# One-hots of a graph score pass from squares: VectorE compares on broadcast rows become TensorE products and ScalarE Relu

## The reference, cut to what matters

```python
Q, K = enh @ Wq + bq, enh @ Wk + bk          # one row per node
mod_k  = K[src] + 0.2 * rel_w[edge_relations][:, None, :]
scores = einsum('ehd,ehd->eh', Q[dst], mod_k) / D ** 0.5
```

## Time and profile before

| | |
|---|---|
| median of three runs | 2750.49 us (2748.61 to 2753.2) |
| span of the profiled execution, first to last instruction | 2465.8 us |
| busy in the span | PE 86%, DVE 73%, POOL 60%, ACT 35% |
| score pass, by window 214.00 to 1294.50 | 1080.5 us |
| TensorE clock granted in the score pass, mean | 0.83 |
| bytes moved in the score pass | 348 GB/s |

### The profile page before, as it was taken

The page is one execution under the profiler, slowest core; times in us unless marked ns, Lnnn a source line. Parts: engine busy times, 40 slices in busy tenths (PEclk is TensorE's granted clock), DMA queues, the critical chain, the costliest instruction groups (busy, mean ns, idle before and its releaser), DMA issues. The chain is left out here.

```text
span 2465.8 us, 50459 instructions
## 1 busy us (share of the span) xinstructions
PE 2121.3 (86%) x11360; PEld 1390.5 (56%) x11361; DVE 1790.9 (73%) x3103; ACT 863.0 (35%) x2796; POOL 1476.9 (60%) x1460
## 2 busy tenths in 40 slices
PE   6994888888888888888856999999789999779996
PEld 3542444444444444444425877777655555468885
DVE  6666999999999999999957777888776665331111
ACT  3541111111111111111106777777535555432221
POOL 3665777777777777777731777777664441024342
PEclk9996888888888888888868999999989999889998
DMA  5666999999999999999995988888534552465451
GB/s 174 210 208 187 358 360 358 365 354 359 364 354 352 358 360 359 354 360 358 359 207 194 315 278 282 278 278 280 195 128 154 194 192 104 162 234 183 151 178 42
DMA packets 387966, 649.65 MB, mean 263 GB/s; under 512 B 40218, under 2 KB 235806, under 8 KB 387780
## 3 DMA queue, kind: packets, MB, share of 16 engines
q1 hardware_dynamic: 309812, 386.36, 46.9%
q0 software_dynamic: 77824, 262.55, 30.2%
q10 hardware_dynamic: 272, 0.00, 0.0%
HBM read 470.87 MB, written 178.83 MB: 263 GB/s over the span
## 5 line engine op out<-in xcount | busy, mean ns | idle before, releaser
L758 POOL DMA_INDIRECT s_kv<-kv_d,s_index x832 | 793.3, 953 | 266.0 <-issue 247.4
L890 PE MATMUL s_q_ps<-q,s_is_dst 128*128 x2496 | 470.7, 303 | 155.1 <-DVE s_key L812 142.5
L1390 PE MATMUL a_sum_ps<-a_w,a_is_dst 128*128 128x260 f32 x1760 | 402.9, 387 | 20.9 <-DVE sums L1361 11.9
L1303 POOL TENSOR_TENSOR a_w<-a_v,a_w 128x512 f32<-128x512 f32 x220 | 299.1, 1365 | 164.6 <-ACT a_w L1260 109.7
L1390 PEld LDWEIGHTS a_sum_ps<-a_w,a_is_dst 128*128 128x128 f32 x1760 | 327.4, 190 | 96.4 <-issue 26.0
L890 PEld LDWEIGHTS s_q_ps<-q,s_is_dst 128*128 128x128 bf16 x2496 | 200.6, 102 | 285.4 <-issue 226.7
L808 DVE TENSOR_TENSOR s_key<-s_kv,s_rel_ps 128x1024 f32<-128x1024 f32 x208 | 252.5, 1214 | 53.1 <-DMA s_kv<-kv_d,s_index 46.5
L1276 ACT ACTIVATE a_w<-a_v,a_w 128x64 f32<-128x64 f32 x1100 | 285.8, 335 | 2.8 <-DMA a_v<-v_d 2.8
L1337 DVE SCALAR_TENSOR_TENSOR a_is_dst<-node_of,first_node,a_col_ps 128x256 f32<-128x256 f32 x440 | 208.5, 475 | 83.0 <-PE a_sum_ps L1390 65.8
L817 DVE TENSOR_REDUCE s_part<-s_key 128x16 f32<-128x1024 f32 x208 | 253.7, 1220 | 10.7
L812 DVE TENSOR_TENSOR s_key<-s_key,s_q_ps 128x1024 f32<-128x1024 f32 x208 | 253.8, 1220 | 7.2
(11 more groups left out here) (312 smaller groups left out, 2942.1 us busy)
## 6 DMA issues: line engine op xcount, KB each, us to landing
a_v<-v_d SPq DMA_DIRECT2D x440, 256.0 KB, 3.7
v_d<-s_kv SPq DMA_DIRECT2D x208, 512.0 KB, 8.2
s_local<-local_d SPq DMA_DIRECT2D x106, 256.0 KB
...
s_kind<-type_d SPq DMA_DIRECT2D x212, 64.0 KB
s_kv<-kv_d,s_index POOLq DMA_INDIRECT x832
kv_d<-pkv SPq DMA_DIRECT2D x50, 256.0 KB, 2.0
...
```

What stands on the lines that cost most here:

```text
L758: nc.gpsimd.indirect_dma_start(out=kv[:, g * GROUP + b, :], out_offset=None, in_=R["kv"], in_offset=bass.IndirectOffsetOnAxis(ap=index[:, ...
L890: nc.tensor.matmul(q_ps[b][:, u, :], is_dst[:, h, e], M["q3"][:, bass.ds(regs[g % GROUPS * GROUP + u], 1), j, :] .rearrange("p a c -> p (a ...
L1303: nc.gpsimd.tensor_tensor(heads(w[:, at, mine, 0:C]), heads(v[:, g, mine, :]), w[:, at, mine, C:, None].broadcast_to([P, len(tiles), H, D] ...
L1390: ins = nc.tensor.matmul(sum_ps[(g * PAIRS + k) % BANKS][:], is_dst[:, g % WRING, 2 * k + u, :], w[:, g % WRING, 2 * k + u, :], start=(u = ...
```

## The change

Neither `local` nor `type` is broadcast any more. The identity used is relu(1 - (lane - value)^2), which for whole numbers is 1 where they are equal and 0 elsewhere. The square is written as lane^2 - 2 lane value + value^2, and value^2 is split into a bf16 part and its rest, so that three bf16 rows per number (`terms`: high square, low square, value) carry it exactly. TensorE multiplies these rows (6 partitions, `s_marks`, both numbers together) by a constant matrix `M["mark"]` into `s_off_ps`, and ScalarE applies Relu with the bias `M["slack"]` = 1 - lane^2.

- `stage_weights`: 14 small VectorE instructions make `mark` and `slack`.
- `stage_tiles`: the rows for both numbers are squares and rests, made by DVE, ACT and POOL; 6 rows per 8 tiles are stored, 624 KB for each number, instead of 208 KB.
- `stage_scores`: VectorE's compares are gone. SP fetches 12 KB of `s_marks` for 8 tiles (four sets in flight), instead of 384 KB. Per group, PE makes two more products of 512 columns (`mark_kind`, `mark_dst`) and ACT two Relu of 128x512. `s_rel_ps` and `s_off_ps` are one buffer each: each mark waits until ACT has read the one before, and the relation product waits until DVE's add of the group before has read `s_rel_ps` (`key_added`). The first two relation parts are stacked on 128 partitions, so a tile has 2 relation products (L976 with 128 rows, L977 with 64) instead of 3. ACT's indices come one or two groups later, and its squares of the mixer are spread over two groups.

```diff
@@ stage_weights, VectorE @@
+            lane, a_dst, b_dst, a_kind, b_kind = M["lane"][:], *(coef[:, j:j + 1] for j in range(4))
+            st.mark(nc.vector.tensor_scalar(a_dst, lane, 1.5, None, ALU.is_lt))
+            st.mark(nc.vector.tensor_scalar(b_dst, lane, 2.0, -2.0, ALU.is_equal, ALU.mult))
...
+            st.mark(nc.vector.tensor_tensor(M["slack"][:, 0:1], lane, lane, ALU.mult))
+            st.mark(nc.vector.tensor_tensor(M["slack"][:, 1:2], M["lane64"][:], M["lane64"][:], ALU.mult))
...
+            st.mark(nc.vector.tensor_scalar(M["slack"][:], M["slack"][:], -1.0, 1.0, ALU.mult, ALU.add))
+            st.settle()
+            st.mark(nc.vector.tensor_scalar(M["mark"][:, 0, :], M["col"][:], b_dst, a_dst, ALU.mult, ALU.add))
+            st.mark(nc.vector.tensor_scalar(M["mark"][:, 1, :], col64[:], b_kind, a_kind, ALU.mult, ALU.add))
+            st.settle()
...
-            for j, part in enumerate((rel_1, rel_2, rel_3)):
-                st.mark(nc.vector.tensor_copy(M["rel3"][:, j, :], part[:]))
+            st.mark(nc.vector.tensor_copy(M["rel3"][0:NREL, 0, :], rel_1[0:NREL, :]))
+            st.mark(nc.vector.tensor_copy(M["rel3"][NREL:, 0, :], rel_2[NREL:, :]))
+            st.mark(nc.vector.tensor_copy(M["rel3"][0:NREL, 1, :], rel_3[0:NREL, :]))
 
@@ stage_tiles: SyncE, GpSimd, VectorE, ScalarE @@
-            for name, tile, ready in (("type", type_b, "type_set"), ("local", local_b, "local_stored")):
-                sp.wait_ge(S[ready], 1)
-                sp.dma_start(R[name][0:TS_ROWS, :], tile[:]).then_inc(S["stored"], 16)
-                sp.dma_start(R[name][TS_ROWS:, :], tile[0:2, :]).then_inc(S["stored"], 16)
+            for lo, ready in ((0, "near"), (MARK, "type")):
+                sp.wait_ge(S[ready + "_high"], 2)
+                sp.wait_ge(S[ready + "_low"], 1)
+                part = slice(lo, lo + MARK)
+                sp.dma_start(R["rows"][0:TS_ROWS, part, :], terms[:, part, :]).then_inc(S["stored"], 16)
+                sp.dma_start(R["rows"][TS_ROWS:, part, :], terms[0:4, part, :]).then_inc(S["stored"], 16)
...
+            pool.wait_ge(S["type_set"], 1)
+            nc.gpsimd.tensor_tensor(type_sq[:], type_f[:], type_f[:], ALU.mult).then_inc(S["type_squared"], 1)
+            pool.wait_ge(S["type_squared"], 1)
+            pool.wait_ge(S["type_high"], 2)
+            nc.gpsimd.tensor_tensor(term(MARK + 1), type_sq[:], term(MARK), ALU.subtract).then_inc(S["type_low"], 1)
...
+            nc.vector.tensor_scalar(near[:], local[:], -1.0, float(P), ALU.max, ALU.min).then_inc(S["near_set"], 1)
+            dve.wait_ge(S["near_set"], 1)
+            nc.vector.tensor_tensor(near_sq[:], near[:], near[:], ALU.mult).then_inc(S["near_squared"], 1)
...
+            dve.wait_ge(S["near_squared"], 1)
+            dve.wait_ge(S["near_high"], 2)
+            nc.vector.tensor_tensor(term(1), near_sq[:], term(0), ALU.subtract).then_inc(S["near_low"], 1)
...
-            nc.scalar.copy(by_tile(type_b), field(2)).then_inc(S["type_set"], 1)
+            nc.scalar.copy(type_f[:], field(2)).then_inc(S["type_set"], 1)
+            act.wait_ge(S["near_squared"], 1)
+            nc.scalar.copy(term(0), near_sq[:]).then_inc(S["near_high"], 1)
+            nc.scalar.copy(term(2), near[:]).then_inc(S["near_high"], 1)
...
-            act.wait_ge(S["local_set"], 1)
-            nc.scalar.copy(by_tile(local_b), local[:]).then_inc(S["local_stored"], 1)
+            act.wait_ge(S["type_squared"], 1)
+            nc.scalar.copy(term(MARK), type_sq[:]).then_inc(S["type_high"], 1)
+            nc.scalar.copy(term(MARK + 2), type_f[:]).then_inc(S["type_high"], 1)
@@ stage_scores @@
-        rel_ps = [ctx.enter_context(nc.psum_tensor(f"s_rel_ps{b}", [P, 2 * GROUP, D], F32)) for b in range(2)]
+        rel_ps = ctx.enter_context(nc.psum_tensor("s_rel_ps", [P, 2 * GROUP, D], F32))
+        off_ps = ctx.enter_context(nc.psum_tensor("s_off_ps", [P, GROUP * P], F32))
...
-                sp.dma_start(local[:, h, :], row(R["local"], n)).then_inc(rows_in[h], 16)
-                for k in range(2):
-                    sp.dma_start(kind[k * NREL:(k + 1) * NREL, h, :],
-                                 R["type"][bass.ds(n, 1), k * GROUP * P:(k + 1) * GROUP * P]
-                                 .broadcast_to([NREL, GROUP * P])).then_inc(rows_in[h], 16)
-
-            def block_in(n):
-                sp.dma_start(xnt[:], R["xnt"][bass.ds(n, 1)].rearrange("a p c -> (a p) c")).then_inc(xnt_in, 16)
-
-            for h in range(2):
+                sp.dma_start(marks[:, h, :], R["rows"][bass.ds(n, 1)].rearrange("a k e -> (a k) e")).then_inc(rows_in[h], 16)
+
...
-                act.wait_ge(gathered[g], (i + 1) * (16 * GROUP))
+                act.wait_ge(gathered[g], i * (16 * GROUP))
                 act.nop(nofuse=True)
-                indices(g, i + 1)
+                indices(g, i)
+
+            def hot_dst(m, count):
+                act.wait_ge(S["marked"], count)
+                act.nop(nofuse=True)
+                nc.scalar.activation(is_dst[:, m % 2, :], off_ps[:], ACT.Relu, bias=M["slack"][:, 0:1], scale=-1.0
+                                     ).then_inc(S["hot_ready"], 1)
...
+                for g in range(RING):
+                    n, at = i * 2 + g // 4 + 1, (i * RING + g) * 2
+                    hot_kind(g + 1, at + 4)
+                    if g % 4 == 1:
+                        square_keys(n)
+                    if g % 4 == 2:
+                        square_values(n)
+                    if g % 4 == 3:
+                        values(n)
+                        deviation(n)
+                    hot_dst(g + 2, at + 5)
+                    if g < 2:
+                        next_indices(g + RING - 2, i)
+                    elif more:
+                        next_indices(g - 2, i + 1)
+                    if g % 2 == 0 and g > 0:
+                        scores(g // 2 - 1, i)
...
-            def onehots(h, n):
-
-                dve.wait_ge(rows_in[h], n)
-                nc.vector.tensor_scalar(is_dst[:, h, :], local[:, h, :], M["lane"][:], None, ALU.is_equal)\
-                  .then_inc(S["steps"], 1)
-                nc.vector.tensor_scalar(is_kind[:, h, :], kind[:, h, :], M["lane64"][:], None, ALU.is_equal)\
-                  .then_inc(S["onehot_ready"], 1)
-
...
+            def mark_dst(m, seen):
+
+                pe.wait_ge(S["hot_ready"], seen)
+                pe.nop(nofuse=True)
+                nc.tensor.matmul(off_ps[:], M["mark"][0:2 * MARK, 0, :],
+                                 marks[:, m // 2 % SETS, m % 2 * GROUP * P:(m % 2 + 1) * GROUP * P],
+                                 start=True, stop=True).then_inc(S["marked"], 1)
...
+                    b, at = g % 2, i * RING + g
                     if g % GROUPS == 0:
                         regs = load_row(pe, at_block, M["blk"][0:1, bass.ds((i * RINGS + g // GROUPS) * SLOTS, SLOTS)], RBLK - 1)
-                    if b == 0:
-                        pe.wait_ge(S["onehot_ready"], i * (RING // 2) + g // 2 + 1)
-
-                    pe.wait_ge(S["qr_free"], i * RING + g + 1)
+                    mark_kind(g + 1, at * 2 + 3)
+
+                    pe.wait_ge(S["qr_free"], at + 1)
                     pe.nop(nofuse=True)
                     for u in range(GROUP):
-                        e = slice((b * GROUP + u) * P, (b * GROUP + u + 1) * P)
+                        e = slice(u * P, (u + 1) * P)
                         for j in range(3):
-                            nc.tensor.matmul(q_ps[b][:, u, :], is_dst[:, h, e],
+                            nc.tensor.matmul(q_ps[b][:, u, :], is_dst[:, b, e],
                                              M["q3"][:, bass.ds(regs[g % GROUPS * GROUP + u], 1), j, :]
                                              .rearrange("p a c -> p (a c)"), start=(j == 0), stop=(j == 2))
-                        half = slice(b * NREL, (b + 1) * NREL)
-                        for j in range(3):
-                            ins = nc.tensor.matmul(rel_ps[b][:, u, :], is_kind[half, h, u * P:(u + 1) * P],
-                                                   M["rel3"][half, j, :], start=(j == 0), stop=(j == 2))
+
+                    if g % 2 == 0:
+                        pe.wait_ge(rows_in[(g + 2) // 2 % SETS], (i + 1 + (g + 2) // RING) * 16)
+                    mark_dst(g + 2, at * 2 + 4)
+
+                    pe.wait_ge(S["key_added"], at + RING)
+                    pe.nop(nofuse=True)
+                    for u in range(GROUP):
+                        e = slice(u * P, (u + 1) * P)
+                        nc.tensor.matmul(rel_ps[:, u, :], is_kind[:, b, e], M["rel3"][:, 0, :], start=True, stop=False)
+                        ins = nc.tensor.matmul(rel_ps[:, u, :], is_kind[0:NREL, b, e], M["rel3"][0:NREL, 1, :],
+                                               start=False, stop=True)
```

136 lines of the change are left out of this document (81 added, 55 removed).

## The result

The changed kernel takes 3018.85 us, median of 4 runs (3007.98 to 3024.06), beside 2751.84 us (2748.61 to 2756.59) for the kernel before: a ratio of 1.0967, 95% interval 1.0942 to 1.0992. The change makes the kernel 267 us slower; 2738 us were forecast, and 2789 us was the worst rival.

What follows compares the result with a forecast made beforehand. The score pass was taken as bound by DMA throughput, GpSimd's gather issue 3% behind. Tile stage +8.4 us and end of pass -20.9 give -12.5: span 2453.3 plus 284.7 held outside it, 2738 us; range 2727 to 2762.

Steps and rivals of the forecast that it cites:

- Sum: Whole kernel: span 2465.8 us falls by 12.5 to 2453.3; 284.7 us outside it are held, giving 2738 us.
- The pass is bound by DMA throughput: Score pass: DMA engines at 1.01 of their time set the end, GpSimd's issue of gathers 3% behind.
- the 33 us behind the last gather: End of score pass: a DMA backlog that shrinks to 10 to 15 us; 1059 against 1079.9 us, -20.9 us.
- Rival 2: Score pass: traffic was not the bound, the pass keeps 1080 us, the tile stage adds 8.4: 2759 us; chance 0.07.
- TensorE: Score pass: added marks and 0.4 us of waits take its half-turn from 17.4 to 19.6 us, under GpSimd's 20.12.
- Rival 1: Score pass: TensorE becomes the bound through waits on ScalarE and a halved clock, half-turn 21.2 us: 2789 us; chance 0.17.
- Rival 4: Score pass: gathers get shorter without VectorE's compares, 832 x 7 ns = 5.8 us off the train: 2732 us; chance 0.08.
- Traffic: Score pass: about 41 MB of 376 MB of broadcasts go, leaving 966 us of DMA, under GpSimd's 1046 us.
- VectorE: Score pass: the compares L767 and L769 go, 91.6 us, leaving 885 us; room only, no gain of its own.
- ScalarE: Score pass: 416 Relus of 597 ns add 248 us to 151, covered by idle time; indices should not be late.
- Single buffer: Score pass: the relation product waits for VectorE's add one group earlier; 2.4 us against 0.5 to 0.8 needed, costs nothing.
- Tile stage: Before the score pass: making and storing the new rows moves the first gather to about 224.0, +8.4 us (+7 to +12.5).

Runs made afterwards that it cites:

- experiment 1: The kernel before, unchanged, run and profiled again: 2750.78 us, ratio 1.0008; the profiled execution took 2748.0 us, 2.1 us of it outside the span.
- a_plain: The changed kernel with GpSimd's indirect gathers replaced by as many plain transfers at fixed addresses: 2606.79 us, where the kernel before takes 2469.25.
- a_each: The changed kernel with GpSimd waiting for TensorE's products ahead of every group, not every second: 2630.54 us, ratio 1.0654 to the kernel before at 2469.25.
- b_plain: The kernel before with indirect gathers replaced by as many plain transfers at fixed addresses: 2403.63 us, where the unchanged kernel before takes 2469.25.
- b_gap: The kernel before with a 128x128 zero fill on GpSimd after each gather: 2551.16 us, ratio 1.0332 to the unchanged one at 2469.25.
- a_nomarks_plain: The changed kernel with plain transfers for the gathers and without the pass's marks and Relus: 2395.05 us, where the kernel before takes 2746.62.
- b_each: The kernel before with GpSimd waiting for TensorE's products ahead of every group, not every second: 2705.52 us, ratio 0.9851 to the unchanged one at 2746.62.

## Why the prediction was wrong

**The step that failed** is the one under "Sum": "284.7 us of the median of 2750.5 lie outside the span and are held". They do not lie outside (experiment 1). A number that an argument holds constant needs as much of a reason as one it changes; a gap of 10% between a profiled execution and its median was a sign that the trace shows another regime than the runs, and the forecast was made for that regime. In the timed one the DMA engines are at 0.86 and not 1.01, GpSimd's train is in pieces, and TensorE's word is what all wait for. On a chip without the hold a second step fails, "PE's half-turn of 906/52 = 17.4 us becomes 19.6 us, under POOL's 20.12": it takes 22.8 us in a_plain and 23.3 in a_each.

**What bounds the kernel.** On the second kind the issue of the gathers does set the time: with the traffic unchanged and only the issue cheaper, b_plain gains 66 us, and with a dearer issue b_gap loses 82. "The pass is bound by DMA throughput" does not hold even there: in b_plain as many bytes, at fixed addresses, move at 376 GB/s in the 500 us from 300, and at 359 in the trace that the prediction read. Nor were the 33 us behind the last gather a backlog of the DMA engines, from which the sum took -20.9 us. In a_each, on the second kind, with a DMA share of 0.84 in those 500 us, they are still 25.2 and not 10 to 15:

```profile
1423.06 0.94 POOL L822 DMA_INDIRECT s_kv<-kv_d,s_index  x1 [0.30 <-issue]
...
1449.23 0.53 POOL L1064 MEMSET x_pairs<- 128x512 f32 x1 [25.23 <-POOLq L658]
```

Four of VectorE's key additions start behind that gather, some 5 us apart, and four in the trace: GpSimd is that many groups ahead, and they are still to be scored. The forecast counted one. In the changed kernel the next stage begins 31.2 us behind the last gather. To this extent Rival 2 was right. On the timed chips the gathers do not set the time.

**TensorE.** "PE's half-turn becomes 19.6 us", 0.4 of it waits, so 19.2 us of work. In a_plain, where nothing is held, a half-turn takes 22.8 us (192 of VectorE's key additions, divided by 48), 89% or 20.2 us of it work and 56.7 us in 500, or 2.6 us, pauses. The start was right: a_nomarks_plain has 85% of 18.8 = 16.0 us, and 17.4 - 1.1 = 16.3 was said. Three terms were too small. A mark takes 0.41 us where 0.36 was taken, 8 x 0.05 = 0.4 us. The clock did not return to full: it is 0.84 in a_plain with TensorE 89% busy, and 0.91 in a_nomarks_plain, and the rest of the work is some 0.9 us longer, which I put down to it (20.2 - 16.0 - 8 x 0.41). The pauses cost 2.6 us and not 0.4. The direction said to be "hidden by 1.7 us of query products" (L934 behind the Relu L756) is 1.1 us of that, 24.2 in 500. The direction that was given 0.4 us (L942 behind the Relu L750) costs nothing that the trace shows; the 1.5 us ahead of L942 are the loading of registers, which the sum has not. Whether the new waits keep that load from being done ahead of need was not tested.

**Rival 1** had the mechanism, "PE becomes the bound", and priced it at 39 us; free of the hold it is 160 (a_each) to 203 (a_plain). On the timed chips a second thing adds to it that no rival named.

**How hold and hand-overs meet.** The kernel before has two buffers for queries and relations and compares made ahead of need, and it spends 281 us on the hold (2750 against 2469). The change puts three serial hand-overs of TensorE's word into every group: mark to Relu, twice, and relation product to add without a spare buffer. Each that falls into a train waits for its end, GpSimd's next train waits for TensorE, and so they run in lockstep, one train of 8 in 15.5 us instead of 13.1 (1614.56 / 104 with the lead-in, 1359.00 / 104 before). The prices are not additive: with shorter trains on the first kind the changed kernel is 28 us above the kernel before, less than the 160 to 203 it costs with no hold at all. The likely reason, argued and not shown, is that the pauses of the hold leave TensorE idle time in which the marks fit.

**Rival 4** came true beside it and doesn't matter, since GpSimd no longer sets the time: without the compares a gather takes 948 ns on average and not the 956 of experiment 1, 6.4 us over 832. There 87 of the 88 gathers over 0.96 us overlap the compare L769; the changed kernel has 2 gathers as long. b_each has the same compares and only 10, so not every one costs something. The Trainium skill (SBUF — State Buffer, "SBUF: two separate sides") says that GpSimd cannot write the descriptors of its DMAs while VectorE runs an operation in a two-port mode. The 87 of 88 agree with it.

**Traffic.** 649.65 MB became 610.18, 39.5 MB less, as said; it buys nothing where the DMA engines have room. **VectorE** fell from 979 to 908 us, 71 and not 92: one compare starts before the other has ended, so that the pair takes 0.66 us in the trace before (1271.28 to 1271.94) and not 0.48 + 0.35. **ScalarE**: a Relu takes 687 ns, not 597; the indices are not late (7.1 us), as said. **Single buffer**: said to cost nothing; 145 us with the hold, 30 without. The sentence's own arithmetic, 2.4 us of slack against 0.8 us of products, left out the way of the signal; what the 30 us are was not looked into.

**Tile stage.** First gather at 227.51, forecast 224.0, bound 228.1. Not all of it is the change's: in experiment 1 the unchanged kernel has it at 216.52, 0.9 us later than in the earlier trace rows. From the end of the relation's cast to the first gather it is 17.8 us, and 7.6 before, so the change adds 10.3 us where 8.4 was said. From the changed kernel's timeline:

```profile
208.08 1.59 ACT L616 CAST t_type_f<-t_meta 104x1024 f32<-104x1024 int32 x1
...
209.76 2.18 POOL L521 TENSOR_TENSOR t_type_sq<-t_type_f 104x1024 f32<-104x1024 f32 x1 [5.34 <-ACT t_type_f L616]
210.22 2.80 DVE L592 TENSOR_TENSOR t_near_sq<-t_near 104x1024 f32<-104x1024 f32 x1
...
227.51 1.01 POOL L823 DMA_INDIRECT s_kv<-kv_d,s_index  x1 [6.82 <-ACT s_index L737]
```

The cast ends 1.7 us later than in the earlier trace rows, before anything of the change has run in this stage (0.9 us later in experiment 1). VectorE's square takes 2.80 us and not 1.23 while GpSimd's product runs beside it, and ends 1.1 us behind that one. That was the upper bound's "POOL and DVE in each other's way". The Trainium skill (SBUF — State Buffer, "SBUF: two separate sides") says that a VectorE operation with two inputs in SBUF and a GpSimd one that reads SBUF need one shared port, and that the second to start waits for the whole of the first. This row agrees.
